# Keeping transposed rows instead of normalised rows, and gathering four groups into side buffers, in a macaron block of two MoE layers around an SSM mixer

## The chip, the cores and the metric

One core of a Trainium2 chip runs the whole computation in one launch. The metric is device time in microseconds (us) of the launch. An element of the machine is named by its queue: PE (TensorE), DVE (VectorE), ACT (ScalarE), POOL (GpSimd) and SP (SyncE, which only issues transfers here).

## What is computed

Input x is 2 x 2048 rows of 256 numbers; the block is `x + 0.5*ffn(ln(x))`, then `x + mixer(ln(x))`, then `x + 0.5*ffn(ln(x))` again. Cut to what matters:

```python
def _L0_ffn_ref(h, gate_w, sg, su, sd, r_gate, r_up, r_down):
    shared_out = swiglu(x, sg, su, sd)                 # every row, 256 -> 512 -> 256
    logits = x @ gate_w.T                              # 8 experts
    top_id, score = argmax(logits), sigmoid(max(logits))
    xs = x * score[:, None]
    # each row goes through its one expert, 256 -> 512 -> 256
    return shared_out + sum_e swiglu(where(top_id == e, xs, 0), r_gate[e], r_up[e], r_down[e])

def _L0_attn_ref(x, W_in, b_in, conv_w, conv_b, A, Bp, Cp, Dp, W_out, b_out):
    u = causal_depthwise_conv4(x @ W_in + b_in) + conv_b
    h_t = tanh(A) h_{t-1} + u_t Bp ;  y_t = Cp.h_t + Dp u_t   # 16 states a channel
    return silu(y) @ W_out + b_out
```

## The kernel before

**Tiling.** Rows are handled in 32 tiles of 128, as 8 groups of 4 tiles (512 rows, 512 KB). `acc` holds the running x of all rows in SBUF. Products are made of three passes on split numbers (a "hi" part rounded by ACT, a "lo" remainder by DVE; `mm3`, L397 to L401).

**Stages, in the order of PE.** (1) Start: for each group DVE or ACT normalises `acc` into `xg` (two places, L1114 and L1185), PE transposes `xg` into two PSUM banks (`transposes`, L456, with the matmuls recorded at L466), ACT copies the banks to the single buffer `xTf` (`xt_copy`, L869), and PE makes the routing logits from `xTf` (L470, L476). Interleaved are the weights' split, the recursion's constants, and the shared FFN of group 0. (2) Shared FFN of four groups ("half 0", `shared`, L516, DVE's side `shared_group`, L1320). A group is 48 gate and up matmuls of 512 columns, then 48 down matmuls of 256. Meanwhile DVE and POOL choose experts and compute for each row its place in an expert-sorted array, and POOL scatters the rows there, one tile to an indirect transfer (L1773 to L1780). (3) Routed FFN: 39 slots of 128 sorted rows, expert by expert (`routed_slots`). (4) Shared FFN of the last three groups ("half 1"). (5) The mixer, 8 blocks n = 0 to 7 in the order of `group_of(n)` = 0, 4, 1, 5, 2, 6, 3, 7 (`attention` on each engine; `mix_chunk(0, ...)` of block 0 stands inside the last group of half 1, L541 to L544). (6) The second FFN layer, by stages 2 to 4 again, then the last gathers and the stores of the output.

**Order of groups.** `ORDER[0]` is (0, 7, 1, 2, 4, 5, 6, 3): group 0 in the start, 7, 1, 2, 4 in half 0, 5, 6, 3 in half 1. `ORDER[1]` is (6, 7, 0, 1, 2, 3, 4, 5).

**The normalised rows.** SP stores each group's `xg` to `xn_dram` (`keep`, L1995), 8 times a layer. They are read back twice: six groups a layer into `xg` for the shared FFN (`shared_load`, L2044), where PE transposes them again (`shared_transposes`, L567, called at L530, L539 and L648, eight matmuls a group), and eight groups a layer into `rows` (`load_rows`, L2035), where DVE multiplies them by the score (`scale_rows`, L1386) and POOL scatters them. `rows` has two places of four tiles, so a load waits until the scatters of two groups before have landed (L2041). `SCALED` (L1407) says after which quarter `fb` of which group DVE scales which group.

**The gathers.** After the routed stage of the first layer POOL adds each row's expert output to `acc` by indirect gathers with an add in the transfer (`gather`, L1838, L1845): groups 0, 4, 1, 5, 2, 6 ahead of the mixer loop (L1904 to L1916), with the layer norm's small steps `ln2_rsqrt` between them, then group 3 in the loop's first pass (L1943) and one tile of group 7 in each of the next four (L1930). A gather into `acc` waits for `add_shared` of that group. In the mixer loop POOL also adds the convolution's bias (L1750) and makes the lo parts of y (L1754). In the tail of the second layer three groups are gathered plainly into `yr` (L1954) and added by DVE (`add_rows`, L1383).

**Zeroing.** POOL zeroes the sorted array with five large transfers out of `rows` (`zero_slots`, L1683, L1686), issued near the end of the start.

## Time and profile before

| what | us |
|---|---|
| median of 3 runs (lowest to highest) | 887.05 (886.29 to 892.61) |
| the profiled execution | 887.72 |
| span of its profile | 885.9 |
| PE busy in the span | 840.4 |

All times below are counted from the start of the span. The span is 1.8 us shorter than the profiled execution's own time; what lies around it is taken as unchanged. The busy time of PE is modelled, since its matmuls are pipelined: "busy" reaches from the first matmul's start to a modelled end, so gaps under some tenths of a us don't show, and the distance from one start to the next is the better measure.

### The profile page before, as it was taken

How to read it: one execution, taken by the hardware profiler on the slowest of the kernel's cores; microseconds unless marked ns; L12 is line 12 of the kernel's file. 1: busy time of each engine (PE TensorE's matmuls, PEld its weight loads, DVE VectorE, ACT ScalarE, POOL GpSimd, SP SyncE). 2: the span in 40 equal slices, each digit the busy share in tenths (PEclk: the TensorE clock that was granted, in tenths of full speed). 3: DMA queues.
4: the chain of work that ended last, by engine and by line, in shares of the span. 5: the costliest groups of instructions: out<-in, count | busy, mean ns of one | idle time of the engine just before them, and what ended most of it. 6: DMA issues, size and time to landing. Idle time of an engine off the chain costs nothing.

```text
span 885.9 us, 16372 instructions
## 1 busy us (share of the span) xinstructions
PE 840.4 (95%) x5398; PEld 732.2 (83%) x5399; DVE 478.9 (54%) x997; ACT 389.8 (44%) x766; POOL 457.5 (52%) x435
## 2 busy tenths in 40 slices
PE   4899989999999999999998999999999999999993
PEld 3688878888888878888787988988888888888883
DVE  6887733333333336668998886856333333333352
ACT  4743223434343434456676776333334333334230
POOL 5527760333334018879999983577331242330685
PEclk9999999999999999998999999999999999999997
DMA  9795663546464225231111016357445555511566
GB/s 309 239 359 167 232 197 110 195 165 225 148 217 161 88 72 95 41 43 24 30 32 31 25 49 235 108 198 253 152 139 182 201 190 201 187 62 36 108 151 152
DMA packets 72694, 128.66 MB, mean 145 GB/s; under 512 B 6746, under 2 KB 64228, under 8 KB 68292
## 3 DMA queue, kind: packets, MB, share of 16 engines
q0 software_dynamic: 17536, 74.33, 26.7%
q1 hardware_dynamic: 54610, 53.63, 18.9%
q8 instruction: 32, 0.52, 0.2%
q14 instruction: 18, 0.15, 0.1%
q10 hardware_dynamic: 498, 0.02, 0.0%
HBM read 91.64 MB, written 36.32 MB: 144 GB/s over the span
## 4 chain that ended last, share of the span: by engine, by line
PE 72%; POOL 13%; DVE 5%; issue 3%; DMA 3%; ACT 1%; POOLq 0%; DVEq 0%; ACTq 0%; SPq 0%
PE bank L399 21%; PE bank L400 20%; PE bank L401 20%; POOL acc L1845 5%; PE bank L607 4%; PE bank L466 2%; DMA wr_hi<-w_routed 2%; PE bank L576 2%; POOL v L1750 2%; DVE v L1464 2%; POOL wr_lo L1818 1%; POOL yr L1954 1%; POOL hT_lo L1754 1%; POOL xs_sorted L1778 1%; DVE stats L1178 1%
## 5 line engine op out<-in xcount | busy, mean ns | idle before, releaser
L1818 POOL TENSOR_TENSOR wr_lo<-wr_raw,wr_hi 128x3072 fp32r<-128x3072 f32 x14 | 95.3, 6806 | 93.3 <-DMA wr_hi<-w_routed 86.6
L399 PE MATMUL bank<-wr_hi,xT_hi 128*128 x312 | 130.4, 418 | 2.0 <-POOL wr_lo L1818 2.0
L400 PE MATMUL bank<-wr_hi,xT_lo 128*128 x312 | 124.0, 397 | 0.0
L401 PE MATMUL bank<-wr_lo,xT_hi 128*128 x312 | 123.2, 395 | 0.0
L1422 DVE TENSOR_TENSOR hf<-sg,bank 128x512 f32<-128x512 f32 x78 | 53.6, 687 | 126.2 <-PE bank L401 126.2
L1167 DVE TENSOR_TENSOR hT_lo<-bank,hT_hi 128x512 fp32r<-128x512 f32 x78 | 53.9, 691 | 124.7 <-ACT hT_hi L861 124.7
L1845 POOL DMA_INDIRECT acc<-ys_sorted,pos x52 | 85.7, 1649 | 54.5 <-DMA ys_sorted<-rows 40.1
L399 PE MATMUL bank<-xT_hi,ws_hi 128*128 128x512 f32 x256 | 102.3, 400 | 2.2 <-DVE xT_lo L1167 2.2
L400 PE MATMUL bank<-xT_hi,ws_lo 128*128 128x512 f32 x256 | 100.8, 394 | 0.0
L401 PE MATMUL bank<-xT_lo,ws_hi 128*128 128x512 f32 x256 | 100.5, 393 | 0.0
L877 ACT ACTIVATE sg<-bank 128x512 f32<-128x512 f32 x64 | 38.2, 597 | 136.9 <-PE bank L401 123.2
L861 ACT ACTIVATE xT_hi<-bank 128x256 fp32r<-128x256 f32 (+1 forms) x126 | 56.0, 464 | 93.5 <-PE bank L576 87.5
L399 PE MATMUL bank<-wr_hi,hT_hi 128*128 x312 | 93.8, 301 | 1.3 <-DVE hT_lo L1167 1.3
L401 PE MATMUL bank<-wr_lo,hT_hi 128*128 x312 | 87.4, 280 | 0.0
L400 PE MATMUL bank<-wr_hi,hT_lo 128*128 x312 | 87.3, 280 | 0.0
L1778 POOL DMA_INDIRECT xs_sorted<-rows,pos x64 | 64.8, 1012 | 28.5 <-issue 17.5
L1464 DVE SCALAR_TENSOR_TENSOR v<-bank,vec,v 128x511 f32<-128x511 f32 (+2 forms) x96 | 70.9, 746 | 12.9 <-ACT v L1010 10.4
L940 ACT ACTIVATE sg<-bank 128x512 f32<-128x512 f32 x78 | 46.6, 598 | 70.5 <-PE bank L401 70.5
L1269 DVE TENSOR_TENSOR hf<-sg,bank 128x512 f32<-128x512 f32 x64 | 43.6, 683 | 62.4 <-PE bank L401 42.9
L399 PE MATMUL bank<-ws_hi,hT_hi 128*128 128x256 f32 x256 | 74.1, 289 | 0.1
L401 PE MATMUL bank<-ws_lo,hT_hi 128*128 128x256 f32 x256 | 72.8, 285 | 0.0
L400 PE MATMUL bank<-ws_hi,hT_lo 128*128 128x256 f32 x256 | 72.8, 284 | 0.0
(237 smaller groups left out, 2111.8 us busy)
## 6 DMA issues: line engine op xcount, KB each, us to landing
wr_raw<-w_routed POOLq DMA_DIRECT2D x16, 1536.0 KB
wr_hi<-w_routed POOLq DMA_DIRECT2D x16, 1536.0 KB
rows<-xs_sorted SPq DMA_DIRECT2D x78, 128.0 KB, 2.6
ys_sorted<-rows SPq DMA_DIRECT2D x78, 128.0 KB, 1.7
xn_kept<-xg SPq DMA_DIRECT2D x16, 512.0 KB, 3.5
rows<-xn_kept SPq DMA_DIRECT2D x16, 512.0 KB
xg<-xn_kept SPq DMA_DIRECT2D x12, 512.0 KB
acc<-x SPq DMA_DIRECT2D x8, 512.0 KB, 9.8
```

The costliest lines, as they stand in the source:

```text
L399: pe.matmul(o, a_hi, b_hi, start=start, stop=False, skip_group_check=True)
L400: pe.matmul(o, a_lo, b_hi, start=False, stop=False, skip_group_check=True)
L401: return pe.matmul(o, a_hi, b_lo, start=False, stop=stop, skip_group_check=True)
L861: return act.activation(o, i, ACT.Copy)
L940: act.activation(sg[:, 0, :], MG[:, :], ACT.Silu).then_inc(s_msg, 1)
L1167: return dve.tensor_tensor(o, full, f32(h), ALU.subtract)
L1269: dve.tensor_tensor(hf[:, fb % 2, :], sg[:, fb % 2, :], U2[fb % 2][:, :], ALU.mult).then_inc(s_h, 1)
L1422: dve.tensor_tensor(hf[:, 0, :], sg[:, 0, :], MU[:, :], ALU.mult).then_inc(s_mh, 1)
L1464: dve.scalar_tensor_tensor(vb_[:, d:GN], UB[cb % 2][:, 0:GN - d], vec[:, cb, k:k + 1], vb_[:, d:GN], ALU.mult, ALU.add).then_inc(s_tap if ...
L1778: pool.indirect_dma_start(out=xs_dram, out_offset=bass.IndirectOffsetOnAxis(ap=pos[:, tt:tt + 1], axis=0), in_=rows[:, half * GT + t, :], ...
L1818: pool.tensor_tensor(wr_lo[:, e % 2, :], wr_raw[:, :], f32(wr_hi[:, e % 2, :]), ALU.subtract).then_inc(s_wl, 1)
L1845: pool.indirect_dma_start(out=acc[:, tt, :], out_offset=None, in_=ys_dram, in_offset=bass.IndirectOffsetOnAxis(ap=pos[:, tt:tt + 1], axis= ...
```

## The change

Transposed rows `xTf` are stored to DRAM instead of normalised rows, only for the six groups of a layer that need them again; the shared FFN loads them and ACT and DVE split them straight out of SBUF, without a transpose by PE. In the start `xTf` gets a second buffer (`xTf_odd`), and ACT's copy for group g waits until the store of group g-2 has landed (`r1_copy`, `ln3_copy`). The rows to scatter are made by DVE from `acc` (mean, and rstd times score), in the order of `ORDER`, into a ring of five buffers; each group's are made before its `add_shared`. The first of them and the product rstd times score come right before the first `add_shared` of a layer. In the first layer groups 4, 2, 6 and 3 are gathered plainly into `rows` and added to `acc` by DVE (`add_apart`): all POOL's gathers come ahead of the mixer's loop. The core of it:

```diff
         def xTf_r1(g): return (xTf, xTf_odd)[g % 2]
+        KEPT = (ORDER[0][2:], tuple(n_of(g) for g in ORDER[1][2:]))
+        APART = (NH, 2, NH + 2, 3)
@@ PE, shared(L, half)
-                    if L == 1 and half == 0 and first:
-                        shared_transposes(L, groups[1])
                     shared_gu(L, g, 2)
                     shared_gu(L, g, 3)
-                    if not last and not (L == 1 and half == 0 and first):
-                        shared_transposes(L, groups[i + 1])
@@ PE, routed_slots
                 m_transpose_h(L, NS - 1)
-                shared_transposes(L, half_groups(L, 1)[0])
                 m_down(L, NS - 1, now)
@@ ACT
+            def xt_kept_hi(L, g):
+                p = place_s(L, g)
+                if g == half_groups(L, 1)[0]:
+                    act.wait_ge(s_mu, (L + 1) * NS)
+                else:
+                    act.wait_ge(s_u, 4 * c_s(L, g))
+                act.wait_ge(s_xg[p], loaded_s(L, g))
+                for kb in range(KB):
+                    hi(xT_hi[:, kb, :], kept_part(p, kb)).then_inc(s_xh, 1)
+            def r1_copy(g):
+                if g - 2 in KEPT[0]:
+                    act.wait_ge(s_xc[g % 2], stored(0, g - 2))
+                xt_copy(t_r1(g), xTf_r1(g))
@@ DVE
             def ln2_stats(n):
-                wait_apart(dve, s_ga[group_of(n)], 64)
+                if group_of(n) in APART:
+                    wait_apart(dve, s_fad, 1 + APART.index(group_of(n)))
+                else:
+                    wait_apart(dve, s_ga[group_of(n)], 64)
@@ DVE, shared_group
+                    if L == 0 and half == 1 and i == 1 and fb == 0:
+                        add_apart(APART[0])
                     if L == 0 and half == 1 and i == 1 and 1 <= fb <= 2:
                         ln2_stats(fb - 1)
+                    if L == 0 and half == 1 and i == 2 and fb == 2:
+                        add_apart(APART[1])
                     s_mult(L, g, fb)
@@
                 if L == 0 and half == 1 and g == groups[-1]:
+                    add_apart(APART[2])
                     state_lo(0, 0)
                     state_lo(0, 1)
                     mix_lo(0)
@@
+            def add_apart(g):
+                i = APART.index(g)
+                dve.wait_ge(s_ga[g], 16 * GT)
+                dve.wait_ge(s_add, 2 * (c_s(0, g) + 1))
+                dve.tensor_tensor(tiles(acc, g), tiles(acc, g), rows[:, i % 2 * GT:(i % 2 + 1) * GT, :],
+                                  ALU.add).then_inc(s_fad, 1)
+            def scale_rows(L, k):
+                g = ORDER[L][k]
+                if k >= ROW_RING:
+                    dve.wait_ge(s_sct[k % ROW_RING], 64 * row_uses(L, k))
                 for t in range(GT):
-                    ins = dve.tensor_scalar(r, r, score[:, bass.ds(g * GT + t, 1)], None, ALU.mult)
+                    ins = dve.tensor_scalar(row_buffer(k)[:, t, :], acc[:, g * GT + t, :], mv[:, g, t, 0:1],
+                                            rscale[:, g, t:t + 1], ALU.subtract, ALU.mult)
@@
-            SCALED = ([{3: (0,), FB: (1,)}, {1: (2,), 3: (3,)}, {0: (4,), 2: (5,), FB: (6,)}, {1: (7,)}],
-                      [{1: (0,), 2: (1,)}, {1: (2,), 3: (3,)}, {0: (4,), 2: (5,), FB: (6,)}, {1: (7,)}])
+            SCALED = ([{1: (1,), 2: (2,), 3: (3,), FB: (4,)}, {2: (5,), FB: (6,)}, {1: (7,)}, {}],
+                      [{0: (1,), 1: (2,), 2: (3,), FB: (4,)}, {2: (5,), FB: (6,)}, {1: (7,)}, {}])
@@ DVE, mixer loop
+                    if n == 2:
+                        add_apart(APART[3])
@@ DVE, before the first add_shared of each layer
+            row_scales(0)
+            scale_rows(0, 0)
             add_shared(0, 0)
@@ POOL
             gather(0, s_ga[0])
-            gather(NH, s_ga[NH])
+            gather_apart(NH, 0)
             gather(1, s_ga[1])
             ln2_rsqrt(0)
             ln2_rsqrt(1)
             pool.wait_ge(s_add, 2 * (c_s(0, NH + 1) + 1))
             gather(NH + 1, s_ga[NH + 1])
+            gather_apart(2, 1)
             pool.wait_ge(s_step, 16)
             conv_bias(0)
-            gather(2, s_ga[2])
+            gather_apart(NH + 2, 0)
             ln2_rsqrt(2)
-            pool.wait_ge(s_add, 2 * (c_s(0, NH + 2) + 1))
-            gather(NH + 2, s_ga[NH + 2])
+            gather(NG - 1, s_ga[NG - 1])
+            gather_apart(3, 1)
             for n in range(NG + 4):
-                if 1 <= n <= GT:
-                    gather_tile(NG - 1, n - 1, s_ga[NG - 1])
-                if n == 0:
-                    pool.wait_ge(s_add, 2 * NG)
-                    gather(3, s_ga[3])
@@ SP
-            def keep(made, count, place, g):
-                sp.wait_ge(made, count)
-                sp.dma_start(tiles(xn, g), xg[:, place, :, :]).then_inc(s_xc[place], 16)
+            def keep(f, i, src, g):
+                sp.wait_ge(s_xf, 2 * f + 2)
+                sp.dma_start(xt_kept[:, g, :], src[:, :, :].rearrange("p k n -> p (k n)")).then_inc(s_xc[i % 2], 16)
```

`load_rows` with its 16 transfers, `shared_transposes`, and the waits of PE on `s_rsv`, `s_fla` and `s_flv` that stood before it are gone. `zero_slots` reads a tile of its own (`zeros`). `cut_expert(L, 1)` on POOL additionally waits until the last scatters out of the three new row buffers have landed. Means, rstd and shifts of all groups are kept (`mv`, `rstd`, `shift` have 10 places in place of 4).

## Rows read from the trace of the kernel before

**Rows 1.** The page, part 4: the chain that ended last

```profile
PE 72%; POOL 13%; DVE 5%; issue 3%; DMA 3%; ACT 1%; POOLq 0%; DVEq 0%; ACTq 0%; SPq 0%
```

**Rows 2.** Windows of 10 us: length, busy by engine (instructions), clock, DMA share, GB/s

```profile
120.00:130.00 10.00, 6.98 (x51) 6.72 (x50) 3.33 (x6) 1.21 (x3) 6.05 (x2) 0.92 0.43 152
130.00:140.00 10.00, 9.37 (x47) 7.49 (x45) 3.43 (x6) 2.56 (x5) 1.76 (x2) 0.91 0.50 173
...
390.00:400.00 10.00, 6.91 (x48) 6.02 (x46) 9.39 (x20) 7.57 (x18) 6.88 (x5) 1.00 0.16 24
400.00:410.00 10.00, 9.37 (x42) 7.96 (x43) 9.48 (x11) 3.25 (x7) 9.36 (x10) 0.66 0.22 31
```

**Rows 3.** PE's timeline (start us, us): one group's transposes, first layer, half 1

```profile
340.24 1.04 PE L466 MATMUL bank<-ident,xg 128*128 128x128 f32 x8
341.03 0.36 PE L399 MATMUL bank<-ws_hi,hT_hi 128*128 128x256 f32 x1
```

**Rows 4.** DMA issues, KB and median us to landing: all; then the one at 36.55

```profile
xn_kept<-xg SPq DMA_DIRECT2D x16, 512.0 KB, 3.5
...
xn_kept<-xg SPq DMA_DIRECT2D x1, 512.0 KB, 13.5
```

**Rows 5.** End of the start: timelines of POOL, ACT and PE

```profile
32.53 3.90 POOL L1686 DMA_DIRECT2D xs_sorted<-rows  x4
...
38.29 1.06 POOL L1686 DMA_DIRECT2D xs_sorted<-rows  x1
...
38.11 1.08 ACT L873 ACTIVATE xTf<-bank 128x512 f32<-128x512 f32 x2 [1.92 <-PE bank L466]
...
44.62 1.09 ACT L873 ACTIVATE xTf<-bank 128x512 f32<-128x512 f32 x2 [0.93 <-PE bank L466]
...
51.36 0.40 PE L399 MATMUL bank<-xT_hi,ws_hi 128*128 128x512 f32 x1
```

**Rows 6.** Timeline of DVE in group 7 and in group 1 of half 0

```profile
59.74 0.67 DVE L1269 TENSOR_TENSOR hf<-sg,bank 128x512 f32<-128x512 f32 x1
...
64.75 1.28 DVE L1392 TENSOR_SCALAR rows<-rows,score 128x256 f32<-128x256 f32 x4
...
77.68 2.84 DVE L1392 TENSOR_SCALAR rows<-rows,score 128x256 f32<-128x256 f32 x4 [2.75 <-DMA rows<-xn_kept]
```

**Rows 7.** First layer's scatters and first slot: POOL, SP and PE timelines

```profile
66.94 1.29 POOL L1778 DMA_INDIRECT xs_sorted<-rows,pos  x1 [1.33 <-DVE rows L1392]
...
119.58 0.96 POOL L1778 DMA_INDIRECT xs_sorted<-rows,pos  x1 [0.30 <-issue]
...
127.73 0.44 PE L576 MATMUL bank<-ident,rows 128*128 128x128 f32 x2 [3.02 <-DMA rows<-xs_sorted]
```

**Rows 8.** The gathers into acc, as a group: busy us, mean ns, idle before

```profile
L1845 POOL DMA_INDIRECT acc<-ys_sorted,pos x52 | 85.7, 1649 | 54.5 <-DMA ys_sorted<-rows 40.1 <-issue 14.3
```

**Rows 9.** Tail: plain gathers of one group on POOL, and DVE's addition

```profile
865.18 0.99 POOL L1954 DMA_INDIRECT yr<-ys_sorted,pos  x1 [0.31 <-issue]
...
868.99 0.95 POOL L1954 DMA_INDIRECT yr<-ys_sorted,pos  x1 [0.30 <-issue]
...
872.38 1.23 DVE L1383 TENSOR_TENSOR acc<-acc,yr 128x1024 f32<-128x1024 f32 x1 [3.79 <-DMA yr<-ys_sorted,pos]
```

**Rows 10.** POOL, DVE and PE timelines ahead of the mixer and in block 0

```profile
356.96 0.73 POOL L1667 TENSOR_SCALAR ve<-mv 128x4 f32<-128x4 f32 x1 [1.17 <-DVE mv L1182]
...
367.31 3.27 POOL L1712 TENSOR_SCALAR cbs<-step,vec 128x512 f32<-128x512 f32 x4
...
372.89 0.69 DVE L1269 TENSOR_TENSOR hf<-sg,bank 128x512 f32<-128x512 f32 x1 [1.42 <-PE bank L401]
...
376.40 0.36 PE L399 MATMUL bank<-tt_hi,xh 128*128 128x256 f32 x1 [0.93 <-issue]
...
380.89 0.29 PE L399 MATMUL bank<-ws_hi,hT_hi 128*128 128x256 f32 x1
...
399.89 0.51 PE L399 MATMUL bank<-xT_hi,win_hi 128*128 128x512 f32 x1 [3.09 <-DVE xT_lo L1167]
```

More of the change, by code:

```diff
@@ L269, in build @@
         s_scl = sem("rows_scaled")
-        s_rl = [sem("rows_loaded_even"), sem("rows_loaded_odd")]
-        s_sct = [sem("scattered_even"), sem("scattered_odd")]
+        s_rsc = sem("row_scales_done")
+        s_sct = [sem(f"scattered{b}") for b in range(ROW_RING)]
         s_tab = sem("slot_table_done")
@@ L298, in build @@
         s_ga = [sem(f"gathered{g}") for g in range(NG)]
-        s_fin = [sem(f"last_gathered{g}") for g in range(NG)]
         s_fad = sem("gathered_rows_added")
@@ L471, in logits @@
                 pe.wait_ge(s_xf, 2 * f + 2)
+                xTf = xTf_r1(f) if f < NG else xTf_r1(0)
                 for kb in range(KB):
@@ L1325, in shared_group @@
                     if half == 0:
-                        for row_group in SCALED[L][i].get(fb, ()):
-                            scale_rows(L, row_group)
+                        for k in SCALED[L][i].get(fb, ()):
+                            scale_rows(L, k)
                     if L == 1 and half == 1:
@@ L1361, in shared_group @@
                 if half == 0:
-                    for row_group in SCALED[L][i].get(FB, ()):
-                        scale_rows(L, row_group)
+                    for k in SCALED[L][i].get(FB, ()):
+                        scale_rows(L, k)
                 if L == 1 and half == 1:
@@ L1771, in scatter @@
             def scatter(L):
-                for g in range(NG):
-                    half, n = g % 2, L * NG + g
-                    pool.wait_ge(s_scl, n + 1)
+                for k, g in enumerate(ORDER[L]):
+                    pool.wait_ge(s_scl, L * NG + k + 1)
                     for t in range(GT):
@@ L1848, in gather_tile, with gather_apart @@
                     compute_op=ALU.add).then_inc(s, 16)
+            def gather_apart(g, place):
+                i = APART.index(g)
+                if i >= 2:
+                    pool.wait_ge(s_fad, i - 1)
+                for t in range(GT):
+                    pool.indirect_dma_start(
+                        out=rows[:, place * GT + t, :], out_offset=None, in_=ys_dram,
+                        in_offset=bass.IndirectOffsetOnAxis(ap=pos[:, g * GT + t:g * GT + t + 1], axis=0)
+                    ).then_inc(s_ga[g], 16)
             def y_all_stored(L):
@@ L2063, in _ @@
+            kept_load(0, 4)
+            routed_slots(0)
+            kept_load(0, 5)
+            for n in sorted(KEPT[1])[:-1]:
+                keep(f_ln3(n), n, xTf, group_of(n))
+            sp.wait_ge(s_xnl, NG)
+            kept_load(1, 0)
+            n = sorted(KEPT[1])[-1]
+            keep(f_ln3(n), n, xTf, group_of(n))
+            sp.wait_ge(s_xt, 2 * (t_ln3(NG - 1) + 1))
+            for i in range(1, 5):
+                kept_load(1, i)
             routed_slots(1)
-            shared_load(1, 5)
+            kept_load(1, 5)
```

266 lines of the change are left out of this document (124 added, 142 removed).

## The prediction

> **What bounds the kernel now.** I read the page's chain first [rows 1]: PE carries 72% of it and POOL 13%. So two questions decide: what the change takes out of PE's stream, and which waits it removes or makes at the few places where PE is not what ends last. The windows of 10 us find these places [rows 2]: PE is busy 6.98 of 10 us at 120 and 6.91 at 390; from 50 to 870 no other falls under 8. The same rows show a second price of a wait: after the one at 124.7 the granted clock is 0.92 and 0.91 for 20 us, which is 0.17 x 10 = 1.7 us lost, and after the one at 396.8 it is 0.66 for 10 us, 3.4 us lost. Both waits were about 3 us long (3.02 and 3.09) [rows 7, 10]. Last, the tail: POOL issues gathers without a gap from 823.5 to 877.4 and PE is done by 872.4. The span ends with POOL.
>
> **Transposes.** Eight transposes stand 0.79 us apart from the next matmul [rows 3]. Twelve such groups go. The two in the tail give nothing, since POOL ends it. The two at the end of the routed stages give nothing either: there PE goes on to wait for the last slot's hT_lo, and the transposes only filled that wait. Eight remain: three in half 0 and two in half 1 of the first layer, three in half 0 of the second. At 0.8 to 0.9 us each they are worth 7 us at most (0 at least, where DVE is late instead). They are taken below, stage by stage.
>
> **The start: the stores of xTf.** ACT's copy for group 7 now waits until the store of group 5 has landed. That store can be issued only when the copy of group 5 is done, at 38.11 + 1.08 = 39.2 [rows 5]. By then POOL has issued four zeroing transfers of 1 MB from 32.53 on and is issuing the fifth [rows 5]. The SP store of 512 KB issued at 36.55, behind the first four, took 13.5 us to land, where the median of its kind is 3.5 [rows 4]. With the same backlog the store of group 5 lands at 39.2 + 12 = 51.2. The copy of group 7 began at 44.62 [rows 5], so it is 6.6 us late, and everything behind it (its logits, the choice of experts, the transposed rows' split) with it: the next group's first matmul, at 51.36, goes to about 58. Bounds: 0 (a landing of 4 us), and 52.7 - 44.6 = 8.1 (13.5 us). I take 6.6, from the row with the same backlog. PE then idles over 3 us, and the clock costs 1.7 (bounds 0 and 3.4). Together **+8.3**.
> The Trainium skill (DMA: Bandwidth & Descriptors, section on queues, rings and completion order) says that a DMA engine takes turns between the queues that have work, packet by packet. By that rule a store on SP's queue would get half of the bandwidth whatever POOL has queued and land in some 4 us; the sum would be 8.3 us lower. The 13.5 us speak against it here; it is a rival below.
>
> **Group 7 of half 0, first layer.** Here DVE is the busy one. It makes two groups of scattered rows in this group now and will make four (`SCALED`), and the fifth, for group 0, right before. Each is 4 tiles, 1.28 us [rows 6]. Counting from the multiplication at 59.74, with the new ones ahead of quarters 1, 2 and 3, hT_lo of quarter 1 is ready at 67.9 instead of 64.8, while PE without its transposes wants it at 66.2, and so on down the quarters; PE ends the group about 2.1 us later than before, in place of 0.9 earlier. The next two groups gain 0.9 each. Sum of the half: **+0.3** (bounds: -2.7 if DVE hides it, and +3 if the scaling takes the 2.84 us of [rows 6], which stood beside a subtraction of POOL, twice).
>
> **The scatters.** POOL scatters 32 tiles from 66.94 to 120.5 [rows 7], with pauses for the scaled rows, and the last one's landing and the slot's load held PE for 3.02 us at 127.73. Rows are now ready ahead of POOL: 32 x 1.27 + three parts of the weights' subtraction, 2.4 each, + 1.2 for issues = 49 us from 65.7 on, so the end comes at 115, 5.5 us earlier, and the slot at 122. PE arrives at about 125. The wait and its clock loss go: -3.0 - 1.7 = **-4.7** (bounds 0 and -5). All of this shifts together with the start.
>
> **Routed stage, first layer**: one matmul stream, nothing removed: 0.
>
> **Half 1 and the way into the mixer.** PE gains two groups' transposes, -1.8, and so would be done with the last group's gate and up at 373.5. But DVE now has two additions on its way that wait for gathers: group 2 ahead of quarter 2 of the last group, where the multiplication ran at 372.89, and group 6 ahead of the state's split, which `mix_chunk(0, 1)` needs. What POOL does before: the gathers of 0, 4, 1; `ln2_rsqrt` of 0 and 1, which need DVE's statistics of group 4 and so stay where they are (from 356.96, 3.3 us); group 5 (into `acc`, 4 x (1.65 + 0.3) = 7.5 us [rows 8]); then group 2 plainly, 5.1 us at 1.27 a tile [rows 9], from 367.9 to 373.0. The last plain gather of the tail started at 868.99 and the addition at 872.38, 3.4 us on [rows 9]; so group 2 is there at 375.1 and the quarter's multiplication at 376.3 instead of 371.1. The bias comes next, 3.3 us [rows 10], then group 6, from 376.3 to 381.4, there at 383.6; the addition takes 1.2, the state's split 0.4. PE's `mix_chunk(0, 1)` goes on at 385.3 and the down matmuls follow at 386.2, not at 380.89 [rows 10]: **+5.3**, all savings of the half included. PE has idled some 8 us in two pieces, so the clock costs 2 more (bounds 0 and 3.4): **+7.3** (lower bound -1.8, gathers that land in time; upper +9.5). Groups 7 and 3 are gathered behind this, to 396; POOL's first bias addition, at 391.4 before, is then wanted at 397 to 399: no further loss.
>
> **The mixer's blocks.** POOL is rid of eight gathers there, 15.6 us [rows 8]. That is not PE's gain: PE's distances between blocks were 18.2 to 21.1 us against 17.8 in a block without gathers, in sum 6.1 us of gaps in blocks 2 to 5 and 0.8 in block 1. DVE is busy over nine tenths there [rows 2], and gets 1.2 us more in block 2, so I give **-4.5** (bounds -7 and -1). The 3.09 us wait in block 0 [rows 10] has its cause in ACT's and DVE's order and stays, with its clock loss.
>
> **Second layer.** Half 0 again: four groups of rows scaled in its first group plus one ahead of it, where PE would gain 0.8 and DVE's chain makes it lose about 1.9; beside POOL's small steps one scaling there took 2.5 us, so another 1; the other two groups gain 0.9 each. Sum **+1.0** (bounds -2.6 and +4). The scatters there were no bound. Tail: 0; it starts with the last slot's store and lasts 32 gathers.
>
> **Sum**: 8.3 + 0.3 - 4.7 + 7.3 - 4.5 + 1.0 = +7.7 us. On the profiled execution's 887.7 that is 895.4; it stands 0.7 above the median of the runs, so against 887.05 I say **895 us**.
>
> **The rivals.**
> *The stores land in time.* For it: the next store of SP, issued after the zeroing had nearly drained, took 5.8 us; and the new stores write 4 KB in one piece where the old ones wrote 1 KB, so they have a quarter of the pieces. Against: the 13.5 us. Then the sum is 7.7 - 8.3 = -0.6: 886.5. Chance 0.22.
> *Both waits stay away* (the gathers land as PE arrives, and the stores too): then -4.7 - 1.8 - 4.5 + 1.3 = about -10: 877. It needs POOL's gathers a good 10 us earlier than counted, or PE that much later. Chance 0.13.
> *The change helps the mixer but not the start*: gathers in time, stores late: 877 + 8 = 885. Chance 0.12.
> *Half clock carries on*, the side above: after both new idle stretches PE stays at the lower of its two levels (1.2 GHz) as long as the window at 400 shows (3.4 us lost each time, in place of 1.7 and 2), and DVE's scaling takes its upper bound in both first groups (+3 for +0.3, +4 for +1). It decides if PE's idle stretches are longer than the old ones. 895 + 1.7 + 1.4 + 2.7 + 3 = 904. Chance 0.11.
> My forecast has 0.42; its own range is 890 to 900.
>
> **How the numbers follow.** A measurement of this kernel tells about 1% from no change, 878.2 to 895.9. Faster: two thirds of the 877 case (0.09) and a sixth each of the 885 and 886.5 cases, whose own spread is some 8 us (0.05): 0.14. Slower: the 904 case (0.11), a little under half of the forecast's (0.19) and a tenth of the 886.5 case: 0.32. Within: the rest, 0.54. Outside the range lie half of the 877 case and two thirds of the 904 one. The range is 877 to 903.
>
> **What would show it.** Right: ACT's copy for group 7 waits for `xT_kept` and begins near 51; a PE gap of some 5 us around 48 to 53 and a clock under 1.0 after it; no wait for the first slot; an idle DVE near the end of half 1 with the gather of group 2, then group 6, as releaser; POOL without `acc` gathers after 400 in the mixer; L466 x128. Wrong: that copy at its old time (first rival), or `mix_chunk(0, 1)` within 2 us of its old distance from the routed stage's end.

## The result, and the profile after

The changed kernel takes 890.59 us (median of 20 runs, 886.81 to 892.54); the kernel before takes 887.49 (20 runs). The ratio is 1.0030, with a 95% interval of [1.0017, 1.0043]: 3.1 us slower, less than 1%. I had forecast +7.7 us and 895 us. The time lies in the range, but the change is less than half of what I had forecast, and three terms of the sum were well off. The question for the experiments is why.

The profiled execution took 888.36 us (span 886.5, where before had 885.9), 2.2 us less than the median of its kernel, so the two traces together show only +0.6 of the +3.1.

The page: the chain, the transposes that are left on PE, and the gathers into `acc`, which were 52 [rows 8]. The columns are those of [rows 1] and [rows 8].

```profile
PE 68%; DVE 14%; POOL 9%; DMA 4%; issue 3%; ACT 2%; POOLq 0%; DVEq 0%; ACTq 0%
...
L488 PE MATMUL bank<-ident,xg 128*128 128x128 f32 x128 | 18.0, 286 | 1.1 <-DVE xg L1225 1.0 <-issue 0.2
...
L1908 POOL DMA_INDIRECT acc<-ys_sorted,pos x36 | 60.4, 1677 | 50.2 <-DMA ys_sorted<-rows 39.8 <-issue 10.4
```

PE lost four points of the chain, POOL too, and DVE gained nine: where PE was bound by its own stream or by POOL, DVE now stands in between. The transposes are gone (x128, as forecast), and so are POOL's gathers in the mixer's blocks.

Three of the windows of [rows 2] (120, 390, 400), and four more in which PE was busy 9 us or more before:

```profile
40.00:50.00 10.00, 6.52 (x97) 5.41 (x98) 5.42 (x17) 3.81 (x8) 0.00 (x0) 1.00 1.01 356
...
120.00:130.00 10.00, 10.00 (x68) 9.16 (x67) 4.00 (x8) 3.53 (x7) 2.71 (x1) 1.00 0.28 102
...
370.00:380.00 10.00, 5.43 (x25) 4.62 (x24) 4.55 (x6) 3.82 (x7) 8.85 (x9) 0.87 0.23 64
380.00:390.00 10.00, 9.47 (x64) 9.31 (x64) 3.36 (x5) 2.70 (x6) 8.54 (x9) 0.79 0.29 56
390.00:400.00 10.00, 10.00 (x71) 9.18 (x69) 8.37 (x14) 4.79 (x12) 8.02 (x7) 1.00 0.40 80
400.00:410.00 10.00, 7.21 (x31) 5.60 (x30) 9.54 (x18) 6.87 (x16) 7.66 (x8) 0.83 0.00 0
...
560.00:570.00 10.00, 5.79 (x19) 4.28 (x18) 9.88 (x24) 1.75 (x3) 7.83 (x11) 0.83 0.15 52
```

The hole at 120 is filled, the one at 390 now lies at 400, and three new ones are there: at 40 (the stores of the start), at 370 (the additions), and at 560, in the first group of layer two, where DVE is busy 9.88 of 10 us.

The timelines at these places (start us, us; in brackets the idle time before it and what ended that), ACT and PE in the start first, then DVE and PE at the mixer's entry, POOL behind its last gather there, and layer two:

```profile
43.06 1.09 ACT L894 ACTIVATE xTf<-bank 128x512 f32<-128x512 f32 x2 [3.88 <-DMA xT_kept<-xTf]
47.77 1.09 ACT L894 ACTIVATE xTf_odd<-bank 128x512 f32<-128x512 f32 x2 [3.11 <-DMA xT_kept<-xTf_odd]
...
44.29 0.64 PE L499 MATMUL bank<-xTf,gw_f 128*32 128x128 f32 x16 [1.46 <-ACT xTf L894]
...
49.00 0.64 PE L499 MATMUL bank<-xTf_odd,gw_f 128*32 128x128 f32 x16 [1.62 <-ACT xTf_odd L894]
...
53.99 0.40 PE L421 MATMUL bank<-xT_hi,ws_hi 128*128 128x512 f32 x1
...
374.09 1.37 DVE L1437 TENSOR_TENSOR acc<-acc,rows 128x1024 f32<-128x1024 f32 x1 [5.23 <-issue]
...
377.48 0.55 PE L421 MATMUL bank<-tt_hi,xh 128*128 128x256 f32 x1 [4.57 <-issue]
...
383.10 1.23 DVE L1437 TENSOR_TENSOR acc<-acc,rows 128x1024 f32<-128x1024 f32 x1 [4.33 <-DMA rows<-ys_sorted,pos]
...
385.76 0.28 PE L421 MATMUL bank<-ws_hi,hT_hi 128*128 128x256 f32 x1
...
396.92 1.30 POOL L1811 TENSOR_TENSOR v<-v,cbs 128x512 f32<-128x512 f32 x1
...
404.46 0.67 PE L421 MATMUL bank<-xT_hi,win_hi 128*128 128x512 f32 x1 [2.79 <-DVE xT_lo L1196]
...
558.16 3.17 DVE L1448 TENSOR_SCALAR rows<-acc,mv,rscale 128x256 f32<-128x256 f32 x4
...
564.59 0.50 PE L421 MATMUL bank<-xT_hi,ws_hi 128*128 128x512 f32 x1 [4.21 <-DVE hf L1304]
```

The first copy of ACT there is for group 6, the second for group 7. PE waits for ACT's two copies 1.46 and 1.62 us. The additions of groups 2 and 6 wait 5.23 and 4.33 us. The profile names the gather as releaser only for the second; that the first waits for its gather too is read from the order: POOL's last gather of group 2 starts at 371.29, and the addition 2.8 us behind it. The last group's down matmuls start at 385.76.

Where the 0.6 us come from, by marks that both traces have (a mark's shift against before, and what each stage adds to it):

| stage, and the mark that ends it | before | after | shift | stage | forecast |
|---|---|---|---|---|---|
| start: gate and up of group 7 | 51.36 | 53.99 | +2.6 | +2.6 | +8.3 |
| half 0: last downs ahead of the first slot | 120.24 | 124.63 | +4.4 | +1.8 | +0.3 |
| scatters: second slot's expansion transposed | 134.79 | 134.42 | -0.4 | -4.8 | -4.7 |
| routed stage: last hT_lo awaited | 324.82 | 323.68 | -1.1 | -0.8 | 0 |
| half 1 and entry: last group's downs | 380.89 | 385.76 | +4.9 | +6.0 | +7.3 |
| mixer: first gate and up of layer two | 536.46 | 534.00 | -2.5 | -7.3 | -4.5 |
| half 0 of layer two: first slot | 625.60 | 626.58 | +1.0 | +3.4 | +1.0 |
| rest: end of the span | 885.9 | 886.5 | +0.6 | -0.4 | 0 |

### The profile page after: what moved, and what is told of

Read it like the earlier page. It is cut to its first block, busy times and chain, and to the rows that moved or that the text cites. A ratio compares the mean times of both kernels' runs of the same rounds, so it can differ in the third digit from the quotient of the medians.

```text
span 886.5 us, 16203 instructions
## 1 busy us (share of the span) xinstructions
PE 832.7 (94%) x5302; PEld 724.6 (82%) x5303; DVE 493.7 (56%) x1003; ACT 391.9 (44%) x766; POOL 454.8 (51%) x435
## 4 chain that ended last, share of the span: by engine, by line
PE 68%; DVE 14%; POOL 9%; DMA 4%; issue 3%; ACT 2%; POOLq 0%; DVEq 0%; ACTq 0%
PE bank L421 20%; PE bank L422 19%; PE bank L423 19%; POOL acc L1908 4%; DVE v L1521 4%; PE bank L618 4%; DMA wr_hi<-w_routed 2%; PE bank L587 2%; DVE xT_lo L1196 2%; POOL wr_lo L1878 1%; DVE stats L1213 1%; POOL yr L2023 1%; PE bank L488 1%; DVE hT_lo L1196 1%; DMA xT_kept<-xTf_odd 1%
## 5 line engine op out<-in xcount | busy, mean ns | idle before, releaser
L1479 DVE TENSOR_TENSOR hf<-sg,bank 128x512 f32<-128x512 f32 x78 | 53.7, 688 | 125.2 <-PE bank L423 125.2
L1908 POOL DMA_INDIRECT acc<-ys_sorted,pos x36 | 60.4, 1677 | 50.2 <-DMA ys_sorted<-rows 39.8
L871 ACT ACTIVATE xT_hi<-bank 128x256 fp32r<-128x256 f32 (+1 forms) x102 | 43.2, 435 | 97.1 <-PE bank L587 84.1
L423 PEld LDWEIGHTS bank<-wr_lo,xT_hi 128*128 128x128 f32 x312 | 58.7, 188 | 14.1
```

The costliest lines, as they stand in the source:

```text
L423: return pe.matmul(o, a_hi, b_lo, start=False, stop=stop, skip_group_check=True)
L871: return act.activation(o, i, ACT.Copy)
L1479: dve.tensor_tensor(hf[:, 0, :], sg[:, 0, :], MU[:, :], ALU.mult).then_inc(s_mh, 1)
L1908: pool.indirect_dma_start(out=acc[:, tt, :], out_offset=None, in_=ys_dram, in_offset=bass.IndirectOffsetOnAxis(ap=pos[:, tt:tt + 1], axis= ...
```

## The experiments

Every kernel is compared with the kernel before, measured at the same time; "marks" are those of the table, and each comes from one profiled execution. Shifts between two edited kernels are read from marks. A ratio of an edited kernel has an interval of some 2 us to each side, so totals that differ by less say little by themselves. All edits start from the changed kernel.

**Again, unedited (c0_again).**

> The changed kernel once more, nothing edited. Theory 'waits': PE's gaps stand where they stood, within 0.3 us each: 1.4 and 1.8 us in the start for the stores of the transposed rows, 4.6 us ahead of the mixer's first chunk, 4.2 us in the first group of layer two; the time is 890.6 within 1. Rival 'chance': the gaps of the first trace were one execution's, and half of their sum (12 us) comes out elsewhere or is missing here; then no one of them can be charged to an edit.

Measured: 888.79 us, ratio 1.0017 [0.9995, 1.0039]; that is 1.8 us under the 890.6, where I had allowed 1. PE's gap for group 7's copy is 1.16 us (group 6's copy no longer leaves one of over 0.3, so half of what I expected of the start is missing), the mixer's is 4.57 again, layer two's 4.35. The start's mark is at 53.74. The places are right; how the start's 3 us are split is not fixed:

```profile
40.00:50.00 10.00, 8.12 (x99) 6.64 (x100) 5.82 (x20) 4.06 (x8) 0.00 (x0) 0.83 1.01 358
```

In this execution the clock fell to 0.83 at 40 and PE was busy longer (8.12 for 6.52), yet the stage ended at the same mark, because the stores' landing set it (47.5, where it was 47.8). At 370 and 380 the clock was 0.74 and 0.75, for 0.87 and 0.79, and the mixer's second product waited 1.54 us for 0.53. So the clock loss of the entry differs by over a microsecond between executions. That this is a part of the difference between the profiled execution and the median is likely, but no run here shows it.

**Four buffers in the start (a_start4).**

```diff
-        def xTf_r1(g): return (xTf, xTf_odd)[g % 2]
+        def xTf_r1(g): return (xTf, xTf_odd, xTf_c, xTf_d)[g % 4]
...
-                if g - 2 in KEPT[0]:
+                if g - 4 in KEPT[0]:
```
(and a semaphore for each buffer, and a wait of POOL for the store of group 6 ahead of a later load of weights)

> Four buffers for the transposed rows of the start instead of two, so ACT's copies for groups 6 and 7 wait for the stores of groups 2 and 3. Theory 'waits add': both gaps of the start (1.41 and 1.78 us) go, the gate and up matmuls of group 7 start at 51 and not at 53.99, the scatters start 3 us earlier too, and all later marks shift with them: 3.0 us less than the changed kernel in the same call (+-0.8). Rival 'backlog': the zeroing transfers set when the first weights and so the first slot are there; PE's stream shifts by 3 us and waits that long at the first slot (128.9), the total stays within 0.7.

Measured: 884.54 us, ratio 0.9972 [0.9951, 0.9993], 4.3 us less than the unedited kernel measured beside it, a little more than the 3.0 (within 0.8) that I had expected. Both gaps are gone, group 7's gate and up start at 50.09 and not at 53.74, and the first slot's transposes at 125.03 for 128.68: the shift of 3.65 us is carried to the mixer (373.39 for 376.96, 3.6). Nothing took the wait's place; the rival falls.

**The stores in pieces of 1 KB (l_pieces).** This asks why the start cost a third of what I had said.

```diff
-    xt_dram = nc.dram_tensor("xT_kept", (NG * P, KB * GN), F32, kind="Internal").ap()
-    xt_kept = xt_dram.rearrange("(g p) f -> p g f", p=P)
+    xt_dram = nc.dram_tensor("xT_kept", (NG * 4 * P, KB * GN // 4), F32, kind="Internal").ap()
+    xt_kept = xt_dram.rearrange("(g c p) f -> p g c f", p=P, c=4)
```
(and the patterns of `keep` and `kept_load` to match)

> The transposed rows' stores and loads in pieces of 1 KB in DRAM, as the normalized rows of the kernel before had them, instead of 4 KB; nothing else. It asks why the store of group 5 landed after 9.1 us where I had estimated 12. Theory 'pieces': the same bytes in four times as many pieces get a smaller share beside the zeroing transfers; the stores of groups 4 and 5 land after 12 to 14 us, ACT's copies for groups 6 and 7 begin near 47 and 55, and the gate and up matmuls of group 7 start at 58 to 61: 4 to 7 us more than the changed kernel. Rival 'backlog': the 13.5 us of the row of before were due to what was queued at that moment (it was issued 4 us into the zeroing), the pieces don't matter, and all marks of the start stay within 0.7 us.

Measured: 895.44 us, ratio 1.0109 [1.0091, 1.0128]. ACT's copies in it (timeline), and the landing of group 5's store in this kernel and, in the next fence, in the changed one (DMA issues of 38.5 to 38.8 us: KB, us to landing):

```profile
47.63 1.08 ACT L894 ACTIVATE xTf<-bank 128x512 f32<-128x512 f32 x2 [8.54 <-DMA xT_kept<-xTf]
53.26 1.08 ACT L894 ACTIVATE xTf_odd<-bank 128x512 f32<-128x512 f32 x2 [4.03 <-DMA xT_kept<-xTf_odd]
...
q1 hardware_dynamic: 2583, 2.57, 32.0%
...
xT_kept<-xTf_odd SPq DMA_DIRECT2D x1, 512.0 KB, 14.6
```

```profile
q1 hardware_dynamic: 821, 3.01, 31.3%
...
xT_kept<-xTf_odd SPq DMA_DIRECT2D x1, 512.0 KB, 9.1
```

Group 7's gate and up start at 59.48, 5.5 us later than in the changed kernel. The line of SP's queue (q1: packets, MB, share of the engines, 30 to 56 us) says what differs: the changed kernel's 3.01 MB go in 821 packets, this one's 2.57 MB in 2583, for the same share of the engines' time. How the two queues share the engines is seen where both have work all the time. First this kernel from 40 to 48 us, then the changed one from 43.2 to 46.2 (q0 is POOL's queue with the zeroing, q1 is SP's):

```profile
q0 software_dynamic: 558, 2.13, 79.1%
q1 hardware_dynamic: 556, 0.55, 21.4%
```

```profile
q0 software_dynamic: 150, 0.58, 55.6%
q1 hardware_dynamic: 132, 0.51, 46.4%
```

Both queues send nearly the same number of packets. With 4 KB against the zeroing's 4 KB SP's store gets almost half of the bytes, with 1 KB a fifth. So of the 9.1 us of the changed kernel's store only about 4 are its transfer: it was issued at 38.69, and its packets run from 43.1 to 46.8. The store before it, issued at 34.34, has no packet before 38.4 either. That pause of 4.1 to 4.5 us, with 4 KB pieces as with 1 KB (34.25 to 38.3 in this kernel), is the other half of the landing; without zeroing transfers in flight it was 0.8 to 0.9 us (29.44 to 30.26 in the changed kernel). What makes it stays open. In this kernel the store of group 5 also has that of group 4 ahead of it on its own queue until 45.6 or so (an estimate: 512 packets from 38.3 at 70 a us).

With the old pieces a store lands as late as [rows 4] say (13.4 us for that of group 4). That the kernel then takes the 895 us that I had forecast is in part chance: by the ratios it is 7 to 8 us over the changed kernel, of which the start gives 5.5. Half 0 of layer two took 1.8 us more as well, which other kernels show without the pieces (see the open point below), and the other terms of my sum, which were off, cancel here.

**Zeroing later (k_zero_later).** POOL issues the five zeroing transfers behind its last square root.

```diff
-            for i in range(ZERO_STORES - 1):
-                zero_slots(i)
             r1_rsqrt(NG - 1)
-            zero_slots(ZERO_STORES - 1)
+            for i in range(ZERO_STORES):
+                zero_slots(i)
```

> POOL issues all five zeroing transfers at 38 us, behind its last square root, instead of four of them at 32. Theory 'a share of the bandwidth': a store of 512 KB lands in 2.6 us when no zeroing transfer is out and in 8 to 9 us when several are, wherever it stands behind them; so the store of group 4 (issued at 34.3) lands by 38, ACT's copy for group 6 doesn't wait, the first gap of the start (1.41 us) goes, the second (1.78 us) stays or grows to 3, and the gate and up matmuls of group 7 start at 53.3 to 54. Total within 1 us of the changed kernel. Rival 'in order': a store waits for what was queued before it; the store of group 5 (issued at 38.7) then has only as much ahead of it as was issued by then and lands within 4 us, both gaps go, and the total falls by 3 us.

Measured: 891.25 us, ratio 1.0031 [1.0011, 1.0052]. They were issued from 33.6 on (the square root came earlier than I had said). ACT's copy for group 6 did not wait, PE's gap for group 7 grew to 2.92 us, and the mark is 54.58. The store of group 5, issued at 37.99, landed by 46.85, after 8.9 us, though the zeroing had a head start of 4.4 us on it in place of 6.8. That the store does not stand in line behind all that was issued before it is to be read in the changed kernel's own DMA issues of 37 to 39 us:

```profile
xs_sorted<-zeros POOLq DMA_DIRECT2D x1, 896.0 KB, 19.0
```

The last zeroing transfer was issued at 37.7, a microsecond ahead of the store (38.69), and landed after 19.0 us, nine microseconds behind it; in pieces of 1 KB the same two took 15.4 and 14.6. The two queues take turns, and the smaller pieces get the smaller share.

**The additions later (DVE) (b_entry).**

```diff
-                    if L == 0 and half == 1 and i == 2 and fb == 2:
-                        add_apart(APART[1])
...
-                    add_apart(APART[2])
+                    add_apart(APART[1])
                     state_lo(0, 0)
                     state_lo(0, 1)
                     mix_lo(0)
+                    add_apart(APART[2])
```

> DVE's additions of the buffers of groups 2 and 6 moved behind the last multiplication and behind the mixer's first splits; POOL's order stays. Theory 'POOL carries the entry': the mixer's first chunk starts near 373.8 instead of 377.5 and the last group's down matmuls near 378.2 instead of 385.8, but POOL gathers without a pause until 396.9 and adds the first bias only then, so PE waits for the second block and w_in of block 1 starts at 404.5 within 1.5: total -1 to 0 against the changed kernel. Rival 'DVE's order': the additions' place alone held PE; w_in of block 1 starts near 397.5 and the total falls by 6 to 7.6 us.

Measured: 887.94 us, ratio 1.0010 [0.9981, 1.0038], 0.9 us less than the unedited one, which is within the noise. The down matmuls start at 377.24, 8.5 us earlier, with no clock loss up to there. Then PE and POOL:

```profile
402.81 0.79 PE L421 MATMUL bank<-xT_hi,win_hi 128*128 128x512 f32 x1 [8.79 <-DVE xT_lo L1196]
...
396.64 2.48 POOL L1810 TENSOR_TENSOR v<-v,cbs 128x512 f32<-128x512 f32 x2
```

PE's wait is 8.79 us there, in place of 2.79, and the clock behind it is 0.70 in the window at 400, where it was 0.83: POOL's first bias is added at 396.64, as in the changed kernel (396.92). Whoever reads the waits of PE alone would have repaired DVE's order for 8 us and got 1. POOL carried the entry.

**POOL's gathers of groups 7 and 3 in the blocks again (d_entry_later)** (on top of the last).

```diff
-            gather(NG - 1, s_ga[NG - 1])
-            gather_apart(3, 1)
...
+                if 1 <= n <= GT:
+                    gather_tile(NG - 1, n - 1, s_ga[NG - 1])
...
+                if n == 0:
+                    gather_apart(3, 1)
```

> As b_entry, and POOL's gathers of groups 7 (accumulating) and 3 (plain) go behind block 0's bias and into blocks 1 to 4. Theory 'POOL's sum counts': POOL is free for the first bias when it is ready, w_in of block 1 starts near 397.5, 5 to 7 us earlier than in b_entry, but the same 12.6 us of gathers then stand in blocks 0 to 4, where POOL is busy over nine tenths, and the gain is given back: the gate and up matmuls of layer two start within 1.5 us of b_entry's. Rival 'only the order counted': POOL has room in the blocks, and 5 us of it are kept to the end.

Measured: 891.54 us, ratio 1.0041 [1.0016, 1.0066]. `w_in` of block 1 starts at 398.58, 4.2 us earlier, and layer two's first gate and up at 536.98, 4.7 us later than in the kernel without this edit (532.27). The blocks gave back twice what the entry gained, more than the 1.5 us that I had allowed. In layer two's half 0 this execution took another 3 us, of which below.

**All gathers into `acc` as before (e_noapart).**

```diff
-        APART = (NH, 2, NH + 2, 3)
+        APART = ()
...
-            gather_apart(NH, 0)
+            gather(NH, s_ga[NH])
```
(and the other gathers and waits of the entry and the blocks as in the kernel before)

> All gathers of the mixer's entry accumulate into the residual again, in the places that they had in the kernel before; the transposed rows, their stores and the scattered rows stay as changed. Theory 'POOL's gathers': the waits of the entry go (first chunk near 372.8, w_in of block 1 near 399, 5.5 us earlier than in the changed kernel), and the gaps of blocks 2 to 5 come back, 7 us, because POOL again carries eight tiles of gathers there; total +1.5 us against the changed kernel (0 to +3). Rival 'ACT's freed wait': the blocks got faster since ACT no longer waits in each block for the store of the normalized rows; then the blocks stay at their new pace without the buffers and the total falls by 5 us.

Measured: 886.81 us, ratio 1.0002 [0.998, 1.0023]. `w_in` of block 1 starts at 396.39 (404.46 in the changed kernel), and the blocks' gaps are back; layer two's first gate and up start at 533.53. From the routed stage's end to that mark it takes 210.15 us, the changed kernel 210.32. So the buffers and additions gain 7 to 8 us in the blocks and lose as much at the entry: by the marks this part of the change is worth nothing. The total came out at the kernel before's, where I had said 1.5 us over the changed one. Against the changed kernel that is 1.3 to 2.5 us less (ratio 1.0002 for 1.0017 and 1.0030), which the noise does not separate from nothing. The clock stays at 1.00 at 370, but this lies inside the 210 us that came out equal, so it does not explain the total; that stays open. The rival, that the blocks got faster from ACT's freed wait, falls.

**POOL's work shortened (h_five).** Group 5 is gathered plainly, into the half of `v` that block 1 writes first, and ahead of the two square roots.

```diff
-            ln2_rsqrt(0)
-            ln2_rsqrt(1)
-            pool.wait_ge(s_add, 2 * (c_s(0, NH + 1) + 1))
-            gather(NH + 1, s_ga[NH + 1])
-            gather_apart(2, 1)
+            gather_apart(NH + 1)
+            ln2_rsqrt(0)
+            ln2_rsqrt(1)
+            gather_apart(2)
```
(with DVE's additions of 5 and 2 ahead of quarters 2 and 3 of the last group, that of 6 behind `mix_lo(0)`, and a wait of ACT for the addition of 5 ahead of block 1's first use of `v`)

> POOL's work ahead of the mixer is shortened by 5.6 us: group 5 is gathered plainly too, into the half of v that block 1 needs first, and before the two square roots, for which POOL paused 3.2 us; DVE adds the groups 5, 2 and 6 where it idles. Theory 'POOL carries the entry': the first bias of the mixer is added near 391 instead of 396.9, w_in of block 1 starts near 398.8, and the total falls by 5 us (4 to 6) against the changed kernel. Rival 'DVE carries it too': with 1.2 us more of additions DVE holds w_in of block 1 at 402 or later, and the total falls by 2 at most.

Measured: 882.82 us, ratio 0.9943 [0.9921, 0.9966], by the ratios 6.6 to 7.7 us under the changed kernel, where I had expected 4 to 6. The first bias is at 389.34, and `w_in` of block 1:

```profile
397.50 0.50 PE L427 MATMUL bank<-xT_hi,win_hi 128*128 128x512 f32 x1 [2.79 <-DVE xT_lo L1204]
```

That is 7.0 us earlier than in the changed kernel, and layer two's first gate and up (527.09) keep 6.9 of it. In half 0 of layer two this execution took 3 us more again.

**The order alone (m_order5).** Group 5 still accumulates, but ahead of the square roots (on top of the later additions).

```diff
-            ln2_rsqrt(0)
-            ln2_rsqrt(1)
             pool.wait_ge(s_add, 2 * (c_s(0, NH + 1) + 1))
             gather(NH + 1, s_ga[NH + 1])
+            ln2_rsqrt(0)
+            ln2_rsqrt(1)
```

> As b_entry, and POOL gathers group 5 (accumulating, as in the changed kernel) before the two square roots and not behind them; it takes h_five's gain of 6.9 us apart. Theory 'POOL's sum': the pauses of 2.4 and 0.8 us ahead of the square roots go, POOL reaches the first bias 3.2 us earlier (393.7), and w_in of block 1 starts 3 us earlier than in b_entry: -3 us; the other half of h_five was the shorter gather. Rival 'the square roots are needed': their results come 6 us later (363 instead of 358), ACT's first normalized rows of the mixer with them, ACT holds the last group's silu, and PE gets a new gap of 2 to 4 us there: total as b_entry or worse.

Measured: 883.36 us, ratio 0.9965 [0.9952, 0.9977]. The first bias is at 392.38, `w_in` of block 1 at 398.60, 4.2 us before that of the later additions alone. ACT waited for the square root until 360.01, with no gap of PE behind it. Layer two's first gate and up start at 528.01: 6.0 us before the changed kernel's, most of h_five's 6.9. Of these 1.7 belong to the additions moved out of the way (532.27), and 4.3 to the exchange, where I had expected 3.

**The scaled rows spread over three groups (c_spread).**

```diff
-            SCALED = ([{1: (1,), 2: (2,), 3: (3,), FB: (4,)}, {2: (5,), FB: (6,)}, {1: (7,)}, {}],
-                      [{0: (1,), 1: (2,), 2: (3,), FB: (4,)}, {2: (5,), FB: (6,)}, {1: (7,)}, {}])
+            SCALED = ([{2: (1,), FB: (2,)}, {1: (3,), FB: (4,)}, {0: (5,), 2: (6,), FB: (7,)}, {}],
+                      [{2: (1,), FB: (2,)}, {1: (3,), FB: (4,)}, {0: (5,), 2: (6,), FB: (7,)}, {}])
```

> The scaled rows spread over three groups in both layers: two groups' rows instead of four in the first group. Theory 'DVE-bound groups': the gaps of 1.29, 1.25 and 0.96 us in layer one and of 4.37 us in layer two, with its clock loss of 1.7, go. In layer one the first slot is then due 3.5 us earlier while the scatters end when they did, which hides 2.4 us of it; sum -2.4 - 6 = -8 (-5 to -9). Rival 'rows late': POOL pauses for rows as in the kernel before, the first slot of layer one waits 3 us again with its clock loss, and the total falls by 3 us at most.

Measured: 886.74 us, ratio 0.9992 [0.9971, 1.0012], 2.1 us less than the unedited kernel, where I had expected 5 to 9. In layer one it is as expected: from group 7's gate and up to the second slot's transposes 77.3 us, for 79.4. In layer two the gap stayed:

```profile
557.98 3.16 DVE L1448 TENSOR_SCALAR rows<-acc,mv,rscale 128x256 f32<-128x256 f32 x4
...
563.11 0.79 PE L421 MATMUL bank<-xT_hi,ws_hi 128*128 128x512 f32 x1 [3.07 <-DVE hf L1304]
```

One scaling, the first, takes 3.16 us, while POOL works out the rows' places, and stands ahead of the first multiplication. Most of the expected 6 us had hung on rows that were not the bound.

**The first scaling behind the first multiplication (i_k0late)** (on top of the last).

```diff
-                scale_rows(1, 0)
-                add_shared(1, g)
...
                     s_mult(L, g, fb)
+                    if L == 1 and half == 0 and i == 0 and fb == 0:
+                        scale_rows(1, 0)
+                    if L == 1 and half == 0 and i == 0 and fb == 1:
+                        add_shared(1, ORDER[1][0])
```

> As c_spread, and in layer two the first group's rows are scaled, and group 6's shared result is added, behind the first and the second multiplication of group 7 instead of ahead of both. Theory 'what DVE does ahead of the first multiplication': c_spread kept 3.23 us of the gap of 4.37, which is the 3.17 us that the first scaling takes beside POOL's small steps; now the gap is 1.0 or less and the clock loss behind it is gone too: 4 us less than c_spread (3 to 5). Rival 'POOL's contention': DVE's work beside POOL's steps stretches wherever it stands, the gap moves one quarter back with over 2 us, and the total is within 1.5 of c_spread.

Measured: 883.11 us, ratio 0.9956 [0.9938, 0.9974], by the ratios 3.2 us less than with the spread alone (the two were not measured at the same time). Its DVE:

```profile
558.97 0.69 DVE L1304 TENSOR_TENSOR hf<-sg,bank 128x512 f32<-128x512 f32 x1
559.57 2.72 DVE L1452 TENSOR_SCALAR rows<-acc,mv,rscale 128x256 f32<-128x256 f32 x4
```

The scaling is nearly as slow as it was, and nobody waits for it: PE has no gap over 0.5 us in that group. From group 7's gate and up to the first slot the half takes 67.0 us, for 71.8 in the changed kernel and 68.0 before.

**The four together (j_all)** (the buffers, POOL's work, the spread, the first scaling).

> The four edits that gained, together: four buffers in the start (a_start4), POOL's shorter work ahead of the mixer (h_five), the rows spread over three groups (c_spread), and the first scaling of layer two behind the first multiplication (i_k0late). Theory 'the waits add': -3.1 (start) -2.1 (layer one, half 0) -6.9 (into the mixer and through it) -4.8 and another 3.0, which h_five lost in layer two's first groups beside POOL: about 18 us less than the changed kernel at 889, that is 871 (868 to 875), a ratio to the kernel before of 0.982. Rival 'what one edit frees, the next one uses': the first slot of layer one, due 5 us earlier, waits for the scatters (3 us and a clock loss of 1.7), and DVE, with additions of 1.2 us in half 1, holds the mixer: 876 or more.

Measured: 871.56 us, ratio 0.9811 [0.9778, 0.9844]: 16 us under the kernel before, by the ratios 18 to 19 under the changed one, and half a microsecond from the sum. The chain, and the windows where the holes were:

```profile
PE 77%; DVE 9%; POOL 7%; issue 2%; DMA 2%; ACT 1%; POOLq 0%; DVEq 0%
...
40.00:50.00 10.00, 9.60 (x125) 8.56 (x124) 8.33 (x24) 6.46 (x10) 0.00 (x0) 1.00 1.01 342
...
370.00:380.00 10.00, 10.00 (x80) 9.77 (x80) 5.05 (x8) 3.61 (x7) 8.36 (x8) 1.00 0.36 50
...
390.00:400.00 10.00, 8.39 (x36) 7.23 (x37) 9.70 (x14) 5.90 (x13) 7.94 (x9) 0.66 0.00 0
...
560.00:570.00 10.00, 10.00 (x47) 8.33 (x46) 7.61 (x13) 2.83 (x6) 8.28 (x8) 1.00 0.41 132
```

One hole is left: the wait of block 0, about 3 us, which [rows 10] had already, with its clock loss (0.66).

Left open: why half 0 of layer two takes 74.8 us and not 71.8 in the executions of h_five and d_entry_later. Their edits can't be the whole of it: k_zero_later, whose program there is the changed kernel's, took 74.1, l_pieces 73.7, and m_order5 71.9. All four slow executions have a lower granted clock in that stretch, and a second wait of PE for DVE of 0.9 to 1.4 us. The half in the changed kernel, then in k_zero_later (length, busy by engine, clock, DMA share, GB/s):

```profile
554.70:626.60 71.90, 67.50 (x375) 58.83 (x375) 52.69 (x98) 21.57 (x38) 47.97 (x46) 0.98 0.38 130
```

```profile
555.00:629.30 74.30, 68.71 (x377) 59.63 (x376) 53.30 (x99) 21.81 (x38) 47.62 (x46) 0.95 0.38 126
```

Whether the clock brings the wait or the wait the clock is not shown. In the four edits together neither wait was left.

## Why the prediction was right, and where it was not

**The start (+8.3; +2.6).** The mechanism was right: ACT's copy for group 7 waits for the store of group 5, and behind it everything. The step that failed is the landing, "the store of group 5 lands at 39.2 + 12 = 51.2". I took it from a store of the same bytes under the same backlog, and left aside that it went in pieces of 1 KB, though I had named that difference under the rival. It landed after 9.1 us, at 47.8, so the copy was 3.15 us late and not 6.6. The run in pieces of 1 KB gives 14.6 us and moves the start's mark by 5.5: the row was good for the pieces that it showed. The second part of the term, 1.7 us for the clock, came to nothing. PE waited 1.46 and 1.62 us, not 5 in one piece, and the clock was 1.00 in the profiled execution; where it fell in executions of the same start (0.83 in c0_again, 0.66 in b_entry), the mark was at 53.7 and 53.3, no later than 53.99.
The Trainium skill (DMA: Bandwidth & Descriptors, the section on queues, rings and completion order) has a DMA engine take turns between queues packet by packet. The traces agree: beside the zeroing the two queues sent 558 and 556 packets in pieces of 1 KB, and 150 and 132 in pieces of 4 KB. What I made of it, half of the bandwidth, holds for pieces of the same size only. And it is the rate of the transfer, 3.7 us for the 512 KB, not the landing, before which the 4.5 us without a packet stand. So the rival that rested on the rule, the stores land in time, was half right: it had named the pieces, but the copy still waited 3.11 us.

**Half 0 of layer one (+0.3; +1.8).** DVE bound group 7, as said (PE waited 1.13, 1.10 and 0.80 us for it). The group took 22.81 us where it had taken 19.86: 2.95 more, where I had counted 2.1. The next two groups gained 1.2 together, not 1.8.

**The scatters (-4.7; -4.8).** Right in mechanism and size: 120 to 130 is full, and no clock is lost.

**Half 1 and the entry (+7.3; +6.0).** The marks were close: I had the additions end at 376.3 and 384.8 and PE's downs at 386.2; they came at 375.5, 384.3 and 385.8, where the stages ahead had shifted the kernel by -1.1. (Four accumulating gathers at 1.65 + 0.3 are 7.8 us, not the 7.5 of the text; they took 8.4.) What I had wrong is what this was worth. I priced DVE's waits as if PE's later marks hung on them; POOL's unbroken work up to 396.9 set the mark that counts (404.46), and removing DVE's waits alone gave 0.9 us. My sentence on the first bias ("wanted at 397 to 399: no further loss") was true only because DVE was late as well: with DVE on time PE waited 8.79 us for it.

**The blocks (-4.5; -7.3).** The reason was right (the gathers of POOL were the gaps; putting them back brought the gaps back), the size a little beyond my bound of -7. I had held DVE for the next bound at nine tenths busy; it was not. From `w_in` of block 1 to layer two DVE's work stayed the same, 117.6 and 118.5 us (the third busy time), while the stretch fell from 136.6 to 129.5, before and after:

```profile
399.89:536.46 136.57, 130.81 (x956) 116.35 (x957) 117.61 (x229) 95.26 (x196) 127.77 (x169) 0.98 0.12 30
```

```profile
404.46:534.00 129.54, 128.19 (x956) 115.59 (x957) 118.48 (x230) 96.32 (x198) 117.89 (x162) 0.99 0.07 26
```

POOL had 127.8 of 136.6 us, more than DVE. With the entry it comes to nothing: from the terms, +7.3 and -4.5 and the 1.8 us of transposes that went anyway, the buffers would have cost 4.6 us, and the run without them gives 0.2.

**Layer two (+1.0; +3.4).** The scaling ahead of the first multiplication took 3.17 us, not the 2.5 that I had taken from a neighbour, and PE waited 4.21 us behind it, with a clock of 0.83 in the window after that. I named the lateness and gave it 1.9 + 1; the run that moves it gave 3.2 by the ratios and 4.0 by the marks.

The terms erred by -5.7, +1.5, -0.1, -0.8, -1.3, -2.8, +2.4 and -0.4, in sum -7.2. The start alone makes 5.7 of it. The others add up to only -1.5 because those that were too high and too low cancel, which is luck and not skill. What is left of the whole is 0.6 us between the two traces and 3.1 between the medians.

## What to carry to other kernels

Take the landing time of a new store from a row with the same piece size as well as the same backlog; here four times smaller pieces made 9 us into 15. Where two queues are busy at once, count their packets in a window: it shows who gets which share of the bytes. Before repairing a wait, ask which engine has had no pause up to the next mark: work moved off the path of one engine (gathers out of the blocks) is paid where the same engine is just as full (ahead of them), unless its sum gets shorter or a pause is filled. And an operation known to stretch beside another engine belongs behind the one that the bound engine waits for, even if that splits a step that was written as one.

## What I had not expected of the hardware

- Beside the zeroing, a store of 512 KB landed in 8.3 to 9.5 us in 4 KB pieces and in 13.4 and 14.6 us in 1 KB pieces, and a zeroing transfer issued 1 us ahead of such a store landed 9 us behind it.
- The two queues sent equal numbers of packets (558 and 556 in 8 us) though those of one were four times larger, and a store issued beside the zeroing had its first packet only 4.1 to 4.6 us later, for 0.8 to 0.9 us without it.
- DVE's four scalings of a group, 1.37 us by themselves, took 3.17 and 2.77 us while POOL did small steps on 256 columns; a split of 1.28 us took 3.74 while POOL subtracted 1024 columns and issued scatters. Why, no run here shows.
- A lower clock in the start (0.83 and 0.66 for 1.00 in the window at 40) cost nothing where a landing set the next mark. Of the entry's two waits, in the six kernels with the changed kernel's program there, the first was 4.56 or 4.57 us each time and the second varied from 0.53 to 2.09, with a clock of 0.66 to 0.87 in the window at 370.
